# A two-layer recurrent/attention block: one block ahead of the loop, all sixteen sequences written out, and a perceptron product made by token

## The reference

```python
xn = _layernorm(x)
s = _L0_attn_ref(xn, ...)            # gated linear attention, 16 heads of 16: state = state * exp(g) + v k, out = state q
g = _silu(_L0_ffn_ref(xn, ...))      # 8 experts of 256x64x256, the two with the largest logits, softmax of those two
x = x + s * g
xn = _layernorm(x)
s = _L1_attn_ref(xn, ...)            # softmax over a window of 64 tokens, 16 query heads, 2 key/value heads
g = _silu(_L1_ffn_ref(xn, ...))      # below
x = x + s * g

def _bitlinear(x, w_latent):         # weights to -1, 0, 1 and one scale for each row
    scale = clip(mean(abs(w_latent), axis=1, keepdims=True), 1e-05)
    tern = clip(round(w_latent / scale), -1.0, 1.0)
    return x @ (tern * scale).T
h = _bitlinear(x, w_fc) + gate * (x @ v.T @ fast_b.T @ u.T)   # 256 -> 1024
r = maximum(h, 0.0)
return _bitlinear(r * r, w_proj)                              # 1024 -> 256
```

## Time and profile before

| | |
|---|---|
| median of 3 runs | 3522.17 us (3518.9, 3522.17, 3524.16) |
| the profiled execution | 3520.74 us, its span in the trace 3519.0 us |
| granted TensorE clock, mean | 0.996 |
| PE busy | 3365.3 us (96%), 34556 matmuls |
| weight loads (PEld) | 2272.8 us (65%) |
| DVE / ACT / POOL busy | 2584.2 (73%) / 1868.9 (53%) / 1286.4 us (37%) |
| DMA queue of the kernel | 103.94 MB, 11.3% of 16 engines' span |

### The profile page before, as it was taken

How to read it: one execution, slowest core, us unless ns; L and a number is a source line. 1 busy time by engine, 2 the same in 40 slices (tenths; PEclk the granted TensorE clock), 3 DMA queues, 4 the chain that set the end, 5 groups by cost and what they waited for, 6 DMA issues and landing times. The chain is left out here.

```text
span 3519.0 us, 89054 instructions
## 1 busy us (share of the span) xinstructions
PE 3365.3 (96%) x34556; PEld 2272.8 (65%) x34556; DVE 2584.2 (73%) x6183; ACT 1868.9 (53%) x4135; POOL 1286.4 (37%) x1473
## 2 busy tenths in 40 slices
PE   3999999999999999999989999999999999999998
PEld 2666666666667666666656666666666666766666
DVE  4777877778677776777767777787777867777677
ACT  2365463645636465464654636556364563646546
POOL 3523335242343423425234252333524234342342
PEclk9999999999999999999999999999999999999999
DMA  3101010010100101101010010101001010010100
GB/s 91 26 23 49 11 46 21 20 48 12 48 18 23 45 23 37 23 25 38 23 38 22 26 37 23 49 11 50 18 20 48 13 47 18 23 45 23 37 23 26
DMA packets 98492, 109.71 MB, mean 31 GB/s; under 512 B 21152, under 2 KB 75024, under 8 KB 98064
## 3 DMA queue, kind: packets, MB, share of 16 engines
q1 hardware_dynamic: 98064, 103.94, 11.3%
HBM read 74.01 MB, written 17.30 MB: 26 GB/s over the span
## 5 line engine op out<-in xcount | busy, mean ns | idle before, releaser
L847 POOL TENSOR_TENSOR qx<-qx 128x512 f32<-128x512 f32 x256 | 278.2, 1091 | 685.0 <-ACT qx L1093 684.1
L1223 DVE TENSOR_TENSOR am<-bank,causal 128x512 f32<-128x512 f32 x512 | 328.2, 683 | 42.2 <-PE bank L1597 42.2
L1448 DVE TENSOR_TENSOR sq_lo<-qx,sq_hi 128x512 fp32r<-128x512 f32 x256 | 207.8, 812 | 193.3 <-ACT sq_hi L1072 192.8
L1356 DVE TENSOR_REDUCE row_max<-bank 128x4 f32<-128x384 f32 x512 | 271.9, 549 | 91.9 <-PE bank L1755 91.9
L968 ACT ACTIVATE tanh_g<-bank 128x256 f32<-128x256 f32 x128 | 49.2, 384 | 405.7 <-PE bank L1486 405.7
L1486 PE MATMUL bank<-w_vg,xt 128*128 128x512 f32 x512 | 252.3, 615 | 0.0
L1527 PE MATMUL bank<-xt,w_down 128*128 128x512 f32 x512 | 237.2, 596 | 0.0
L1871 PE MATMUL bank<-sq_hi,pj_t 128*128 128x512 f32 x512 | 214.4, 419 | 16.4 <-DVE sq_lo L1448 9.8
L1365 DVE TENSOR_TENSOR am<-bank,row_max 128x384 f32<-128x384 f32 x384 | 212.8, 554 | 9.8
L1093 ACT ACTIVATE qx<-bank,scale_fc 128x512 f32<-128x512 f32 x256 | 177.7, 694 | 56.2 <-PE bank L1858 56.2
L1012 ACT ACTIVATE am<-am 128x384 f32<-128x384 f32 x384 | 200.2, 526 | 9.8 <-DVE am L1365 3.3
(11 more groups left out here) (261 smaller groups left out, 8740.0 us busy)
## 6 DMA issues: line engine op xcount, KB each, us to landing
g_wide<-gate_rows SPq DMA_DIRECT2D x64, 512.0 KB, 6.4
qt<-in_L_attn_x SPq DMA_DIRECT2D x136, 128.0 KB, 2.2
x<-in_L_attn_x SPq DMA_DIRECT2D x128, 128.0 KB, 2.2
out<-x SPq DMA_DIRECT2D x128, 128.0 KB, 1.7
k<-k SPq DMA_DIRECT2D x96, 128.0 KB, 2.4
x<-in_L_ffn_w_fc SPq DMA_DIRECT2D x1, 1024.0 KB, 5.8
attn<-in_L_ffn_w_proj SPq DMA_DIRECT2D x1, 1024.0 KB, 8.2
w_up<-in_L_ffn_Wu SPq DMA_DIRECT2D x1, 512.0 KB, 6.0
```

The costliest lines, as they stand in the source:

```text
L847: nc.gpsimd.tensor_tensor(sq[:, n % 3, :], relu[:, n % 3, :], relu[:, n % 3, :], ALU.mult)\
L1223: nc.vector.tensor_tensor(am_tiles[:, :, j], bank[3 + j][:].rearrange("p (f e t) -> p f e t", f=2, e=2), causal[:].unsqueeze(1).unsqueeze( ...
L1356: nc.vector.tensor_reduce(row_max[:, j, :], bank[1 + j][:, 0:4 * KW].rearrange("p (h k) -> p h k", k=KW), AX.X, ALU.max, negate=(j == 0)). ...
L1448: nc.vector.tensor_tensor(sq_lo[:, n % 3, :], sq[:, n % 3, :], sq_hi[:, n % 3, :].bitcast(F32), ALU.subtract)\
```

## The change

Six things. (1) `UNROLL` is 16: all sequences are written out and the loop makes one turn. (2) The three blocks ahead of the loop become one. ACT's queue issues the first sequence's loads and the 19 weights that are needed first, SP's the rest; DVE does the statistics of the first sequence, then the ternary weights and the rest in one list, and PE, ACT and POOL follow it by semaphores. (3) `project` makes the product by token: the squares are stationary, the ternary weights are moving, 8 matmuls of 256 columns in place of 4 of 512. `ffn_turn` goes. `ffn_scaled` moves from ACT to DVE and multiplies by `bc_pj`, the scales along the columns on every partition. (4) `veps` of both layers is made by DVE and not by POOL, and the second half of `head_rstd` stands at step 7 in place of 5. (5) At the start of a sequence `first_queries_keys(6)` stands ahead of `cumulate(0)` on PE and ahead of `decays(0)` on ACT. (6) In the attention loop `attention_bias(c - 1)` stands behind the last difference of the chunk, the first `window_values` copy behind the third, the exponentials of the first chunk ahead of the query copies, and the values' turn and the window values have changed banks, with other waits.

```diff
+UNROLL = 16
...
-UNROLL = 8
...
-    ft = kt[:, :, 0:512]
+    ft = kt[:, :, 512:S]
+    spread = sf[:].rearrange("p (o t) -> p o t", o=KD)
...
+    def ffn_part(c):
+        return ft[:, c % 4 // 2, c % 2 * D:(c % 2 + 1) * D]
...
+        dve.wait_ge(s["nst_ok"], at("nst_ok", 2 * NC))
+        nc.vector.tensor_scalar(veps[:], moments[:, :, 1], EPS, None, ALU.add).then_inc(s["nve_ok"], 1)
 
     def head_rstd(pool, part):
 
-        if part == 0:
-            pool.wait_ge(s["nst_ok"], at("nst_ok", 2 * NC))
-            nc.gpsimd.tensor_scalar(veps[:], moments[:, :, 1], EPS, None, ALU.add).then_inc(s["nve_ok"], 1)
-            pool.wait_ge(s["nve_ok"], at("nve_ok", 1))
...
-        elif p == 3:
-            pe.wait_ge(s["f3_ok"], at("f3_ok", 4))
-        else:
+        elif p < 3:
...
+        @block.sync
+        def _(sp):
+            for dst, src in nat_loads:
+                sp.dma_start(dst, src).then_inc(nat_sem, 16)
+            sp.wait_ge(prep, 4)
+            for r in range(4):
+                sp.dma_start(b_nat[32 * r:32 * r + E, :], a["L0_ffn_bu"]).then_inc(b_sem, 16)
+            for dst, src in loads:
+                sp.dma_start(dst, src).then_inc(w_sem, 16)
+            sp.wait_ge(w_sem, 16 * len(loads))
...
+            nc.gpsimd.memset(o_veps[:], 0.0).then_inc(cleared, 1)
+            pool.wait_ge(cleared, 2)
+            for part in range(2):
+                head_rstd(pool, part)
...
+            for c in range(NC):
+                head_stats(dve, c)
...
+            head_moments(dve)
+            dve.wait_ge(nat_sem, 16 * len(nat_loads))
+            dve.wait_ge(cleared, 2)
+            scales(fc_nat[:], scale_fc, MT, D)
+            for m in range(2):
+                ternary(fc_nat, fc_ter, m)
+            for c in range(NC):
+                head_normalise(dve, c)
+            for m in range(2, MT):
+                ternary(fc_nat, fc_ter, m)
...
+            scales(pj_nat, scale_pj, KD, HID)
+            for o in range(KD):
+                link(nc.vector.tensor_copy(spread[:, o, :], scale_pj[:, o:o + 1].broadcast_to([P, P])))
+            dve.wait_ge(first_sem, 16 * len(first_loads))
...
+            for g in range(NG):
+                head_low_split(dve, g)
+            for m in range(KD):
+                ternary(pj_nat, pj_ter, m)
...
+            head_load(act, 0)
+            act.wait_ge(prep, 4)
+            for dst, src in first_loads:
+                act.dma_start(dst, src).then_inc(first_sem, 16)
...
+            tern_out(bc_pj[:], bank[3], D)
...
-                        pool.wait_ge(s["st2"], at("st2", 2 * hi))
-                        nc.gpsimd.tensor_scalar(veps[:, lo:hi], moments[:, lo:hi, 1], EPS, None, ALU.add)\
-                          .then_inc(s["ve2"], 1)
-                        pool.wait_ge(s["ve2"], at("ve2", part + 1))
+                        pool.wait_ge(s["ve2"], at("ve2", hi))
...
-                        if n in (4, 5):
-                            head_rstd(pool, n - 4)
+                        if n in (4, 7):
+                            head_rstd(pool, n // 7)
...
+                    first_queries_keys(6)
                     decays(0)
-                    first_queries_keys(6)
...
-                    def ffn_scaled(g):
-                        act.wait_ge(s["pj_ok"], at("pj_ok", (g + 1) * MT))
-                        if g:
-                            act.wait_ge(s["ftp_ok"], at("ftp_ok", 4 * g))
-                        for o in range(KD):
-                            nc.scalar.activation(ft[:, o, :], bank[5 + o][:], ACT.Identity, scale=scale_pj[:, o:o + 1])\
-                              .then_inc(s["ft_ok"], 1)
-
                     def ffn_tanh(c):
-                        act.wait_ge(s["ftp_ok"], at("ftp_ok", c + 1))
+                        act.wait_ge(s["ft_ok"], at("ft_ok", c // 2 + 1))
                         if c:
                             act.wait_ge(s["f3_ok"], at("f3_ok", c))
-                        nc.scalar.activation(tanh_f[:], bank[ffn_banks[c]][:, 0:D], ACT.Tanh, scale=0.5)\
-                          .then_inc(s["tf2_ok"], 1)
+                        nc.scalar.activation(tanh_f[:], ffn_part(c), ACT.Tanh, scale=0.5).then_inc(s["tf2_ok"], 1)
...
-                        if n == MT + 2:
-                            ffn_scaled(0)
                         if MT + 3 <= n < MT + 7:
                             ffn_tanh(n - MT - 3)
-                    ffn_scaled(1)
...
+                        dve.wait_ge(s["st2"], at("st2", 2 * c + 2))
+                        nc.vector.tensor_scalar(veps[:, c:c + 1], moments[:, c, 1:2], EPS, None, ALU.add).then_inc(s["ve2"], 1)
...
-                            attention_bias(c - 1)
                         maxima(4 * c + 7)
                         shifted(4 * c + 7)
+                        if c:
+                            attention_bias(c - 1)
...
+                    def ffn_scaled(g):
+                        dve.wait_ge(s["pj_ok"], at("pj_ok", (g + 1) * MT))
+                        if g:
+                            dve.wait_ge(s["f3_ok"], at("f3_ok", 4))
+                        for half in range(2):
+                            nc.vector.tensor_tensor(ft[:, half, :].rearrange("p (a d) -> p a d", d=D),
+                                                    bank[5 + half][:].rearrange("p (a d) -> p a d", d=D),
+                                                    bc_pj[:].unsqueeze(1).broadcast_to([P, 2, D]), ALU.mult)\
+                              .then_inc(s["ft_ok"], 1)
...
+                        if n == MT + 2:
+                            ffn_scaled(0)
...
+                    ffn_scaled(1)
...
+                    first_queries_keys(6)
                     cumulate(0)
-                    first_queries_keys(6)
                     first_queries_keys(7)
...
-                        if c >= 4:
-                            pe.wait_ge(s["oc_ok"], at("oc_ok", c))
+                        if c:
+                            pe.wait_ge(s["o2_ok"], at("o2_ok", c))
...
                     def values_turn(c):
 
                         pe.wait_ge(s["oc_ok"], at("oc_ok", c + 1))
-                        if c:
-                            pe.wait_ge(s["s2_ok"], at("s2_ok", c))
-                        else:
-                            pe.wait_ge(s["low_ok"], at("low_ok", 2))
                         for r in range(4):
-                            mm = nc.tensor.transpose(bank[0][:, r * P:(r + 1) * P],
+                            mm = nc.tensor.transpose(bank[7][:, r * P:(r + 1) * P],
                                                      o2_t[:, r].rearrange("p b q -> p (b q)"), ident[:])
                         mm.then_inc(s["xp_ok"], 1)
 
                     def attention_turn(c):
                         pe.wait_ge(s["o2_ok"], at("o2_ok", c + 1))
+                        if c:
+                            pe.wait_ge(s["s2_ok"], at("s2_ok", c))
+                        if c < 3:
+                            pe.wait_ge(s["v2_ok"], at("v2_ok", c + 2))
                         for k in range(KD):
                             mm = nc.tensor.transpose(bank[0][:, k * P:(k + 1) * P], o2[:, k * P:(k + 1) * P], ident[:])
...
+                        for a in range(4):
+                            out = bank[5 + a // 2][:, a % 2 * D:(a % 2 + 1) * D]
                             for part in (sq_hi, sq_lo):
-                                mm = nc.tensor.matmul(bank[5 + o][:], pj_t[:, m, o * P:(o + 1) * P], part[:, n % 3, :],
-                                                      start=(m == 0 and part is sq_hi),
+                                mm = nc.tensor.matmul(out, part[:, n % 3, a * P:(a + 1) * P], pj_t[:, m, :],
...
-                    def ffn_turn(c):
-                        if c % 4 == 0:
-                            pe.wait_ge(s["ft_ok"], at("ft_ok", KD * (c // 4 + 1)))
-                        if c in (4, 5):
-                            pe.wait_ge(s["z_ok"], at("z_ok", c - 3))
-                        elif c >= 2:
-                            pe.wait_ge(s["f3_ok"], at("f3_ok", c - 1))
-                        j = c % 4
-                        for k in range(KD):
-                            mm = nc.tensor.transpose(bank[ffn_banks[c]][:, k * P:(k + 1) * P],
-                                                     ft[:, k, j * P:(j + 1) * P], ident[:])
-                        mm.then_inc(s["ftp_ok"], 1)
```

More of the change, by code:

```diff
@@ L667, in build_program @@
-    with nc.Block() as block:
-        @block.vector
-        def _(dve):
-            for c in range(NC):
-                head_normalise(dve, c)
-            for g in range(NG):
-                head_low_split(dve, g)
+            nc.vector.memset(tanh_g[:, 0:1], 0.0).then_inc(low_done, 1)
             for p in range(NC // 2):
@@ L679, in _, with turn @@
             head_index(dve)
-        @block.gpsimd
-        def _(pool):
-            nc.gpsimd.memset(attn2[:, 0, 0:1], 0.0).then_inc(out_done, 1)
         @block.tensor
         def _(pe):
+            n = 0
```

(41 more changed lines are left out.)

218 lines of the change are left out of this document (90 added, 128 removed).

## The result

The changed kernel takes 3508.69 us (median; 3507.01 to 3509.57) against 3521.47 us before: a ratio of 0.9964, with an interval of 0.9951 to 0.9976. It is faster, by 12.8 us or 0.4%, and 38.7 us slower than forecast; the time lies above the range.

What follows compares the result with a forecast made beforehand. PE, busy 96% of the span, was taken to bound the kernel. From the profiled 3520.7 us, 12.2 for the turn, 26 for the prologue and 12.8 for 16 sequences came off: 3470 us, range 3440 to 3498 (8 in 10).

Steps and rivals of the forecast that it cites:

- The loop's second turn: Start of the loop's second turn: PE's idle 10.46 us and slow first matmul go, 12.2 us saved, once.
- The prologue: Ahead of the loop: DVE goes straight through in one block, loop starts at 54 against 80.16, 26 us saved.
- The product by token: `project`: eight 256-column matmuls a step take about 0.95 against 0.93 us, +0.4 us a sequence; turns go.
- Case D: Rival in `project`: loads of squares as weights are not hidden, +143 us, 3613 us; chance 0.03.
- The steps: Steps 10 and 11: `ffn_scaled` on DVE makes step 11's product 0.4 us later, fewer turns; net −0.25 us a sequence.
- The tail and the seam: Sequence end and next start: a chain of ACT and DVE ends last, so 0, between −2.3 and +0.6 us.
- The state loop: State loop: `veps` adds eight small operations to DVE's full chunk, +0.4 us a sequence.
- The start of the attention: First turned probabilities no longer wait for their copy, made after the first chunk's exponentials: −0.65 us a sequence in the sum.
- Its chunks: Attention chunks: later bias sum saves some 0.35 us in each of three, delays two; −0.3 us a sequence.
- Case C: Rival: DVE's added work makes each sequence lose 0 to 1.5 us, 3482 to 3506 us; chance 0.27 with E.
- E: Rival: the prologue stays bound by its loads, 3496 us; chance 0.27 together with C.

Runs made afterwards that it cites:

- The last experiment: Changed kernel with multiplication one step earlier, two bias sums put back, layer 2's veps on POOL, plus first matrix first on DVE ahead of the loop: 3429.3 us, 0.9744.
- the experiment: Second layer's veps put back on POOL, against the changed kernel with the multiplication by the scales one step earlier (3450.1 us): 3445.6 us.
- run 1: The text given has no run of this name, so no change or time can be told for it.

## Why the prediction was wrong

One term of the sum failed, the one of the steps; the others were right within their bounds or near the number given. The positions below are those of the third sequence, from its first product, in the timelines of both kernels.

- **The loop's second turn**, 12.2 us: 13.8 in the kernel before with 16 written out. Right.
- **The prologue**, 26 us: 80.16 − 56.49 = 23.7. The mechanism was right, DVE's start was 3 us off: I took 11.3, and it was 14.43, behind statistics that waited for the last of the sequence's eight loads. The last experiment bears out that DVE's start moves the loop's start: 7.2 us earlier in DVE, 5.2 in the loop. That the loads land late because more of them share the DMA engines is argued only.
- **The product by token**, +0.4 us in a sequence: the products are 0.12 apart, each with its own load of weights, and a step's eight take 0.94 where the four took 0.93. Case D did not come.
- **The steps**, −0.25 us in a sequence: here it failed, at +2.10. The steps start 0.56 later than before; up to step 9 PE gained 0.46 of that. From there to the end of step 11's hidden values, where one pair of turns is gone, it lost 3.2. The three turned pairs behind that gave 0.6. The forecast had named the wait, `project(8)` for DVE's multiplication, but had the product of step 11 only 0.4 later. Counted from the steps' start it was 1.4 later (190.88 − 188.95 − 0.56), and 1.56 of slow clock came behind it. Three things are wrong in it:
  - The sum itself. The normalisation's end at 698.67, 1 us earlier, and two multiplications of 0.68 give 699.0 and not the 698.4 that I wrote: 0.6.
  - A reading. The last normalisation did not run 1 us earlier but 0.7, counted from the steps' start (188.82 against 188.95 from the first product). DVE was ahead by more than that in steps 6 to 8, and then stood 0.48 for ACT's squares of step 9; its own work was not what bound it there. That is 0.3.
  - The clock, which was in no case of mine: behind the wait the granted clock falls, and PE's next products take 1.6 us longer.

  Together 2.5 us, of which the rest of the term gave 0.2 back: 2.35 off the forecast in a sequence, 38 us in 16, against the 38.7 that it missed. The other misses are of a few us each and of both signs.
- **The tail and the seam**, 0: the tail gained 1.14, and the gates' transposes now wait 1.4 us for ACT, so the parity scores are 1.28 later from the first product: +0.1. Right, and for the reason given: the chain of ACT and DVE ends last.
- **The state loop**, +0.4: +0.30 by the positions, 0.28 by the experiment's time. **The start of the attention**, −0.65 in the sum: −0.65. **Its chunks**, −0.3: −0.38, made of 0.7 lost in two and 1.1 gained in three, as the sum had it.

Case C came nearest in its numbers: a sequence lost 1.5 (1.55 from 213.5 to 215.05), and 3520.7 − 38.2 + 16 × 1.5 is 3506. That is luck more than insight. C rightly said that DVE gets 1.4 us more at step 10, but it named "a late `sq_lo` holds the product" and `f_gates` beside POOL's square. The waits for `sq_lo` did not grow (9.8 to 9.4). `f_gates` from SBUF does meet the square, once in each sequence and not eight times: 16 of its 128 operations take 1.15, the others 0.41 to 0.42. The one of the third sequence:

```profile
690.89 1.15 DVE L1456 SCALAR_TENSOR_TENSOR f_gates<-tanh_f,k 128x256 f32<-128x256 f32 x1
```

No wait of PE behind it is among the large ones. I gave C, with E, 0.27 and let the range end at 3498, two thirds of the way into it; the clock's share put the time past all of it.

The Trainium skill ("TensorE: Matmul & The Clock Gate", Back-to-back issue gap) gives the distance of two matmuls, without what loads of weights may add, as the columns over 1.2 when the clock is low, and over 2.4 plus 2.5 when it is high, in ns: 213 and 109 for 256 columns. The rows have 0.21 and 0.118, so the first agrees and the second is 9 ns more, here with a load for each matmul. I weighed that page's rule on weight loads and not this one.

The rows of before could not have shown the fall of the clock at this place, since PE stood there 0.27 us at most. But they had it at another. Across the loop's turn the first product took 1.22 in place of 0.59, and the granted clock of the kernel before is low behind that start:

```profile
1801.20:1811.00 9.80, 9.78 (x19) 4.35 (x20) 4.26 (x19) 6.86 (x13) 1.70 (x2) 0.83 0.39 113
```

The pitch that follows is 215.1 against 213.5, the same 1.6 us. I counted them as a cost of the turn, without asking where else the change would make PE stand.

## What to carry to other kernels

When work moves from an engine with slack to one that stands in a queue, look at what the receiving engine is waiting for at that place and put the work into that wait; here one step earlier turned a loss of 1.6 us a sequence into a gain of 2.1 by the median pitches (213.5, 215.1 and 211.4). A stall of TensorE has two prices, its length and the slow stretch that may follow: price a new stall with both, and read the granted clock of the stretch behind it before looking for a cause among the instructions. A change of many parts that moves little should be taken apart: one line of it gave all that the whole gave, and one misplaced pair of instructions hid the rest. Add up the times of a chain a second time before you build on it: 0.6 us of this miss was a slip in a sum of three numbers.

## What was not expected of the hardware

The clock's fall is not settled by the length of the stall alone. At the same place of the program a stall of 2.08 us was followed by a stretch at 0.61 to 0.77 in one sequence and by none in another. Behind such stalls of 2.07 to 2.09 us the clock stayed at the upper level in 2 of 16 sequences of the changed kernel and in 5 of 16 of the one with two bias sums put back. Behind the 16 stalls of 1.44 us at this place, in the kernel with the normalisations behind, it never fell. A sequence without the slow stretch is 1.6 us shorter. What decides between the stalls of equal length stays open.
